# Attention with output projection, group norm and a masked 3x3 convolution: projection in three float16 products, statistics gathered over 60 units, mask tables built earlier

## What is computed

```python
x = x + L0(_gn(x), W_qkv, W_out, rel_height, rel_width)
x = x + L1(_gn(x), weight, bias)
```

## Time and profile before

| | us |
|---|---|
| median of 3 runs | 3703.85 |
| the profiled execution, its own time | 3702.19 |
| its span | 3700.4 |
| PE busy (share of the span) | 3491.4 (94%) |
| DVE busy | 3349.1 (91%) |
| ACT busy | 2966.0 (80%) |
| POOL busy | 2575.1 (70%) |

### The profile page before, as it was taken

How to read it: one execution, slowest core, us unless ns; L and a number is a source line. 1 busy time by engine, 2 the same in 40 slices (tenths; PEclk the granted TensorE clock), 3 DMA queues, 4 the chain that set the end, 5 groups by cost and what they waited for, 6 DMA issues and landing times. The chain is left out here.

```text
span 3700.4 us, 127356 instructions
## 1 busy us (share of the span) xinstructions
PE 3491.4 (94%) x51718; PEld 2480.6 (67%) x51718; DVE 3349.1 (91%) x5626; ACT 2966.0 (80%) x5320; POOL 2575.1 (70%) x3344
## 2 busy tenths in 40 slices
PE   0799999998999999999999999999589999999999
PEld 0587777777888888888888888888434444444444
DVE  9699999999999999999999999999789888888887
ACT  0788888887999999999999999998377777777774
POOL 1677777776777777777777777777366666666664
PEclk9999999999999999999999999999799999999999
DMA  8244544443333333333333333333244434344332
GB/s 374 79 132 133 159 134 154 148 139 105 103 103 97 94 98 103 103 97 91 101 103 103 95 91 103 103 100 83 69 160 162 154 146 154 147 154 154 154 154 83
DMA packets 492549, 464.06 MB, mean 125 GB/s; under 512 B 9664, under 2 KB 469312, under 8 KB 469440
## 3 DMA queue, kind: packets, MB, share of 16 engines
q1 hardware_dynamic: 491968, 455.92, 38.4%
HBM read 321.40 MB, written 134.48 MB: 123 GB/s over the span
## 5 line engine op out<-in xcount | busy, mean ns | idle before, releaser
L984 POOL TENSOR_TENSOR sb_tf<-sb_cf 128x1024 f32<-128x1024 f32 x256 | 609.4, 2382 | 392.2 <-DVE sb_tl L966 370.3
L450 PE MATMUL ps_t<-sb_ident,sb_d 128*108 128x128 f32 x4096 | 662.3, 284 | 6.2 <-ACT sb_pt L638 1.9
L600 DVE TENSOR_TENSOR sb_qb<-ps_q,sb_own_head 128x1024 f32<-128x1024 f32 x512 | 621.1, 1213 | 14.9 <-PE ps_q L432 14.9
L470 PEld LDWEIGHTS ps_s<-sb_kf,sb_qb 128*64 128x64 f32 x16384 | 519.1, 138 | 171.5 <-issue 162.9
L719 POOL TENSOR_TENSOR sb_erel<-sb_brel 128x288 f32<-128x288 f32 x512 | 351.5, 686 | 395.6 <-DVE sb_brel L547 394.7
L892 PE MATMUL ps_c<-sb_th,sb_wc_h 128*128 128x512 f16 x1536 | 584.3, 380 | 40.3 <-DVE sb_tl L966 40.2
L470 PE MATMUL ps_s<-sb_kf,sb_qb 128*64 128x54 f32 x16384 | 585.6, 224 | 2.4 <-DVE sb_scores L580 2.4
L892 PE MATMUL ps_c<-sb_th,sb_wc_l 128*128 128x512 f16 x1536 | 583.3, 380 | 0.0
L892 PE MATMUL ps_c<-sb_tl,sb_wc_h 128*128 128x512 f16 x1536 | 583.2, 380 | 0.0
L749 POOL TENSOR_TENSOR sb_zl<-sb_zf,sb_zh 128x396 f16<-128x396 f32 x512 | 481.1, 940 | 83.1 <-ACT sb_zh L702 83.1
L735 POOL TENSOR_TENSOR sb_prod<-sb_rel,sb_shift 128x192 f32<-128x192 f32 x1024 | 502.1, 511 | 0.0
(11 more groups left out here) (117 smaller groups left out, 8228.0 us busy)
## 6 DMA issues: line engine op xcount, KB each, us to landing
sb_xb<-rows SPq DMA_DIRECT2D x128, 780.0 KB, 6.5
sb_xc<-x SPq DMA_DIRECT2D x64, 1280.0 KB, 5.4
sb_x<-rows SPq DMA_DIRECT2D x128, 512.0 KB, 4.1
x<-sb_x SPq DMA_DIRECT2D x128, 512.0 KB, 3.3
out<-sb_oc SPq DMA_DIRECT2D x64, 1024.0 KB, 3.9
sb_abuf<-rows SPq DMA_DIRECT2D x16, 2048.0 KB, 11.7
sb_st<-rows SPq DMA_DIRECT2D x32, 1024.0 KB, 9.3
sb_raw<-wconv SPq DMA_DIRECT2D x1, 576.0 KB, 3.7
```

The costliest lines, as they stand in the source:

```text
L450: last = pe.transpose(ps_t[0:KV, wj * 128:(wj + 1) * 128], d[:, at:at + KV], ident[:])
L470: last = pe.matmul(s_at, qb[:, qc:qc + QB], kf[:, kc:kc + KR], start=True, stop=True)
L600: dve.tensor_tensor(view(qb, 0, 128, vh * QBW + p * NW * QB, [[QB, NW], [QN, HEADS], [1, QN]]), view(ps_q, 0, 128, 0, [[QN, NW], [0, HEADS ...
L984: pool.tensor_tensor(tf[:, k * TF:(k + 1) * TF], view(cf, 0, 128, c0 + ra * W, [[2 * W, PAIRROWS], [1, W]]), view(cf, 0, 128, c0 + rb * W, ...
```

## The change

The output projection: `wo` and `of` become float16 high and low halves. ACT's copy writes the high half `oh`; DVE makes the low half `ol` from `ps_o` and `oh`, in the body of each group right after `x1`, for group n-5; PE makes three products in place of one, and its `ps_o` of the next group waits for `ol` where it waited for `of`.

The statistics of batch 1: a load is now 4 rows (512 KB). Units 0 to 3 take two of them each, units 4 to 59 one each. SP issues it at the end of its body, behind the load of L413, and DVE takes its two pieces at the end of g = 3 of the same unit. The moments of batch 1 follow in unit 60.

The mask: the moments of L0's output for batch 0 are made in unit 70, and its tables in unit 71. Those for batch 1 are made at the start of the convolution's own block, beside its first loads. The zero rows are stored in unit 4. The two blocks between the stages are gone.

```diff
-        wo = sb("wo", C, F32)
+        wo_h, wo_l = sb("wo_h", C, F16), sb("wo_l", C, F16)
...
-        def moments_tables(dve, link, batches, sqrt_done):
+        def moments_tables(dve, link, batches, sqrt_done, edges=True):
...
+            if not edges:
+                return
...
+        def tile_extremes(dve, link, b):
+
+            hs, n = STRIPS // B, TR // B
+            for t, dst, op in ((tmax, ext[0], ALU.max), (tmin, ext[1], ALU.min)):
+                for h in range(2):
+                    link(dve.tensor_reduce(view(dst, 0, 128, b * n * TC + 4 * h, [[TC, n], [1, 4]]),
+                                           view(t, 0, 128, b * n * 8 * SPT + 4 * h, [[8 * SPT, n], [1, 4], [8, SPT]]),
+                                           AX.X, op))
+                part = tiles_of(dst, b)
+                link(dve.tensor_scalar(part, part, mean_t[:, b * hs:b * hs + 1],
+                                       rstd_t[:, STRIPS + b * hs:STRIPS + b * hs + 1], ALU.subtract, ALU.mult))
+
+            link(dve.scalar_tensor_tensor(tiles_of(ext[0], b), tiles_of(ext[1], b), -1.0, tiles_of(ext[0], b),
+                                          ALU.mult, ALU.max))
+
+        def row_tables(dve, link, b, all_channels):
+
+            hs, n, S8 = STRIPS // B, TR // B, CSTRIPS * TC
+            lo, hi = b * S8 // B, (b + 1) * S8 // B
+            rstd = rstd_t[:, STRIPS + b * hs:STRIPS + b * hs + 1]
+            dve.wait_ge(all_channels, 1)
+            link(dve.tensor_scalar(tiles_of(tabs, b), tiles_of(tabs, b), THRESHOLD, rstd, ALU.is_gt, ALU.mult))
+            for q in range(SPT):
+                dve.tensor_copy(view(ctab, 0, 128, S8 + lo + q * TC, [[SPT * TC, n], [1, TC]]),
+                                view(tabs, 0, 128, b * n * TC, [[TC, n], [1, TC]]))
+            dve.memset(ctab[:, lo:lo + TC], 0.0)
+            dve.memset(ctab[:, 2 * S8 + hi - TC:2 * S8 + hi], 0.0)
+            link(dve.tensor_scalar(nmean[:, b:b + 1], mean_t[:, b * hs:b * hs + 1], -1.0, None, ALU.mult))
+            dve.tensor_copy(ctab[:, lo + TC:hi], ctab[:, S8 + lo:S8 + hi - TC])
+            link(dve.tensor_copy(ctab[:, 2 * S8 + lo:2 * S8 + hi - TC], ctab[:, S8 + lo + TC:S8 + hi]))
+            link(dve.tensor_scalar(view(dtab, 0, 128, lo, [[S8, 3], [1, hi - lo]]),
+                                   view(ctab, 0, 128, lo, [[S8, 3], [1, hi - lo]]), nmean[:, b:b + 1], None, ALU.mult))
...
-                    dve.tensor_copy(wo[:], rawn[:, SPANS[1][0]:SPANS[1][1]])
+                    dve.tensor_copy(wo_h[:], rawn[:, SPANS[1][0]:SPANS[1][1]]).then_inc(w_qh, 1)
+                    dve.wait_ge(w_qh, 1)
+                    dve.tensor_tensor(wo_l[:], rawn[:, SPANS[1][0]:SPANS[1][1]], wo_h[:], ALU.subtract)
...
-                    dve.wait_ge(w_qh, 1)
+                    dve.wait_ge(w_qh, 2)
...
-            STW = WS * W
-            st = sb("st", 2 * STW, F32, pb)
...
+            st = sb("st", 2 * (WS // 2) * W, F32, pb)
...
-            of = sb("of", 2 * 1024, F32, pb)
+            oh, ol = sb("oh", 2 * 1024, F16, pb), sb("ol", 2 * 1024, F16, pb)
...
-            FIRST, LOOP = 6, 4
-            STRIPS_1 = STRIPS // B
-            EARLY = STRIPS_1 // LOOP
-            GN = FIRST + LOOP * EARLY
...
+            HALF = WS // 2 * W
+            HALVES = H * W // HALF
+            DOUBLE = 4
+
+            def gathered(u):
+
+                if 0 <= u < DOUBLE:
+                    return (2 * u, 2 * u + 1)
+                return (u + DOUBLE,) if DOUBLE <= u < HALVES - DOUBLE else ()
+
+            MOMENTS = {HALVES - DOUBLE: 1, UNITS // B + 6: 0}
+            MASK = UNITS // B + 7
             GROUP_STEPS = 2 + 5
...
-                    body(u, u // 2, u % 4, some,
-                         (u - FIRST, (u - FIRST) // 2) if FIRST <= u < GN else None, u == GN)
+                    body(u, u // 2, u % 4, some)
...
-                    if stat is not None:
-
-                        row = settled(sp, (stat[0] + STRIPS_1) * WS + PAD)
-                        sp.wait_ge(sem["st_used"], (stat[0] + 1) * PAR)
-                        sp.dma_start(st[:, h * STW:(h + 1) * STW],
-                                     x_in[:, bass.ds(row, WS), :].rearrange("p a b -> p (a b)")
-                                     ).then_inc(st_loaded[h], 16)
...
+                    for k in gathered(u):
+
+                        row = H + k * (WS // 2) + PAD
+                        if k >= 2:
+                            sp.wait_ge(sem["st_used"], 2 * (k - 1))
+                        sp.dma_start(st[:, k % 2 * HALF:(k % 2 + 1) * HALF],
+                                     x_in[:, row:row + WS // 2, :].rearrange("p a b -> p (a b)")
+                                     ).then_inc(st_loaded[k % 2], 16)
+                    if u == DOUBLE:
+
+                        sp.wait_ge(sem["zeroed"], 1)
+                        for row in (0, ROWS + 1):
+                            sp.dma_start(x1_dram[:, row:row + 1, :].rearrange("p a b -> p (a b)"), zrow[:]
+                                         ).then_inc(sem["edges"], 16)
                 units(sp, body)
                 sp.wait_ge(sem["x1_stored"], UNITS * 16)
+                sp.wait_ge(sem["edges"], 32)
...
-                    if moments_due:
-                        pe.wait_ge(sem["gn_agg_done"], 1)
-                        pe.matmul(ps_q[:, 0:2], gsum[:], aggr[:, 2:4], start=True, stop=True
-                                  ).then_inc(sem["gn_sum_done"], 1)
-                        pe.wait_ge(sem["gn_step_done"], GROUP_STEPS)
+                    if due is not None:
+                        pe.wait_ge(gn_sem[due]["agg_done"], 1)
+                        pe.matmul(ps_q[:, 0:2], gsum[:], aggr[:, 2 * due:2 * due + 2], start=True, stop=True
+                                  ).then_inc(gn_sem[due]["sum_done"], 1)
+                        pe.wait_ge(gn_sem[due]["step_done"], GROUP_STEPS)
...
-                            need(pe, sem["of_done"], m)
+                            need(pe, sem["ol_done"], m)
...
                             if g == 0:
-                                pe.wait_ge(sem["of_done"], (u - 1) * GROUPS)
+                                pe.wait_ge(sem["ol_done"], (u - 1) * GROUPS)
                             need(pe, sem["x1_done"], n - 2 * GROUPS)
                             ob = slot % 2
-                            pe.matmul(ps_y[:, 0:QP], wo[:], of[:, ob * 1024 + g * QP:ob * 1024 + (g + 1) * QP],
-                                      start=True, stop=True).then_inc(sem["y_mm"], 1)
+                            for c, (o, w) in enumerate(((oh, wo_h), (oh, wo_l), (ol, wo_h))):
+                                last = pe.matmul(ps_y[:, 0:QP], w[:], o[:, ob * 1024 + g * QP:ob * 1024 + (g + 1) * QP],
+                                                 start=(c == 0), stop=(c == 2))
+                            last.then_inc(sem["y_mm"], 1)
...
-                def stat_pieces(stat, h, first, count):
-
-                    if first == 0:
-                        dve.wait_ge(st_loaded[h], stat[1] * 16 + 16)
-                    for c in range(first, first + count):
-                        dve.bn_stats(stats[:, bass.ds(stat[0] * (PAR * 6) + (UNITS * 6 + c * 6), 6)],
-                                     st[:, h * STW + c * 512:h * STW + (c + 1) * 512]
-                                     ).then_inc(sem["st_used"], 1)
...
+                link = [linker(dve, gn_sem[b]["step_done"]) for b in range(B)]
...
-                        if moments_due and g == 1:
-                            moments_group(dve, link, (1,), ps_q, sem["gn_sum_done"])
+                        if u in MOMENTS and g == 1:
+                            b = MOMENTS[u]
+                            moments_group(dve, link[b], (b,), ps_q, gn_sem[b]["sum_done"])
+                        if on(n - 5, GT):
+
+                            v, vslot, vg = (u - 1, slot - 1, g - 1) if g else (u - 2, slot - 2, GROUPS - 1)
+                            dims = [[QP, PAR], [1, GW * QN]]
+                            dve.wait_ge(sem["oh_done"], n - 4)
+                            need(dve, sem["y_mm"], (v - 1) * PAR)
+                            dve.tensor_tensor(view(ol, 0, 128, (vslot % 2) * 1024 + vg * GW * QN, dims),
+                                              view(ps_o, 0, 128, 0, [[GW * QN, PAR], [1, GW * QN]]),
+                                              view(oh, 0, 128, (vslot % 2) * 1024 + vg * GW * QN, dims), ALU.subtract
+                                              ).then_inc(sem["ol_done"], 1)
...
-                        if stat is not None:
-                            if g != 1:
-                                stat_pieces(stat, h, (0, 4, 1, 2)[g], (1, 0, 1, 2)[g])
-                        if moments_due and g == 0:
-                            moments_sums(dve, link, (1,), sem["gn_agg_done"])
-                        if moments_due and g == 2:
-                            moments_tables(dve, link, (1,), sem["gn_sqrt_done"])
```

(65 more changed lines are left out.)

94 lines of the change are left out of this document (26 added, 68 removed).

## The result

The changed kernel takes 3809.68 us (median of 4 runs, 3807.32 to 3810.1) against 3703.78: ratio 1.0284, 95% interval 1.0267 to 1.0302. It is slower by 106 us. The forecast said 3742, range 3706 to 3792: the sign is right, the size is missed by 68 us and the range too.

What follows compares the result with a forecast made beforehand. TensorE bounds attention, DVE its statistics stretch; after the change DVE bounds all attention. Terms + 3, + 32, + 45, - 34, + 20, - 28.5, + 0.4 make + 38 on 3702.2: 3740, as median 3742 us, range 3706 to 3792.

Steps and rivals of the forecast that it cites:

- T + 5.2: Units 4 to 59: gathered load lands 5.2 us (at most 6.0) after T, the tile minimum's end; DVE waits 1.4 us.
- T + 3.9: Units 4 to 59: the 512 KB load queued ahead of the gathered one lands 3.9 us after the tile minimum's end.
- The estimate of 3.2 us: Gathered load, units 4 to 59: 2.0 us plus bytes at 436 GB/s, 3.2 us from issue, so DVE would not wait.
- Rival 2, the clock: TensorE's clock falls in each gathering unit, PE then needing 21.9 us against DVE's 21.35: + 31, 3773 us; chance 0.07.
- The reduction, 2.60 until its result is used: Mask tables in unit 71: POOL's reduction delays the relative part some 1.5 us, within 7.4 us for the block.
- E + 14.5: After attention: POOL's first row combination starts 14.5 us after E, the last tile minimum's end, instead of 43.0; 28.5 us gained.
- PE's unit goes to 18.5: Attention: three float16 projection products save PE 0.8 us a unit, from 19.30 to 18.5 us (at most 18.85).
- DVE becomes the bound everywhere in attention: With low halves DVE needs 18.76 us a unit, more than PE's 18.5, and 19.96 in units 4 to 59.
- the first one: Units 4 to 59: the gathered load lands in time, 80 us of waits go, 3662 us; chance 0.14.
- The third: Units from 60 on: engines don't even out between groups, a unit takes 19.55 us, + 50, 3792 us; chance 0.09.
- The fourth: Projection: three float16 products cost PE as much as the float32 one, 19.3 us from unit 60, 3776 us; chance 0.04.
- three limits that the prediction set for being wrong: Wait for sb_st under 0.75 us, clock in units 4 to 59 below 0.95, or period from unit 60 19.3 or more.

Runs made afterwards that it cites:

- e4: The changed kernel, with SP waiting until the gathered load has landed before it issues the next load of xb: 3795.99 us, ratio 1.0245.
- e3: The changed kernel with only the projection undone (one float32 product, float32 copy, no low half on DVE): 3771.05 us, ratio 1.018.
- e1: The changed kernel with SP issuing the gathered load right behind the load of xb, at the start of its body: 3684.99 us, ratio 0.9947.
- e2: The changed kernel with POOL's two late partition_all_reduce replaced by a tensor_tensor add of the same columns: 3792.15 us, ratio 1.0232.

## Why the prediction was wrong

In units 4 to 59 the mechanism was right: the order of the queues, the place of the wait and its releaser, and with them the low half (0.34) and DVE's unit with a gathered pair (19.94, forecast 19.96). The waiting there was put too low, and further terms were mis-sized; what bounds the units from 60 on was wrong (point 4).

1. **"It lands at T + 5.2 ... so DVE waits 1.4 us a unit."** Measured 1.93, and 0.53 x 56 = 30 us. The step that failed first is the landing of the load ahead, T + 3.9: I took the median of 20 transfers, where the mean of 52 between 240 and 1280 us of before is 4.14 and single ones reach 5.65. DVE has no reserve, so it pays each transfer's own delay and the mean counts, tail included. In the kernel after the mean is 4.18, which explains about 0.3 of the 0.5. The rest is the load's own part, 1.51 us between the two landings where I had taken 1.3. The load of xb behind has 0.18 in these two together (e4). The estimate of 3.2 us that the prediction took from the Trainium skill, "DMA: Bandwidth & Descriptors", section "Anatomy of one DMA — SWDGE (gpsimd) path", belongs to transfers issued by GpSimd, and these are issued by SP; by the 4.14 us for 512 KB it would have been too low for the load ahead as well. The upper end of my own range for the wait, 2.0, was near; the whole range missed because the other terms below went the same way with it.

2. **Rival 2, the clock.** It was kept apart from the forecast as all or nothing. It came in part: in 23 of 55 units the clock fell to 1.2 GHz, mostly for 3.4 us, and PE's spare time took most of it. Those units are 0.36 us longer besides their wait, 8 us in all, instead of 31; that the lower clock is what lengthens them is argued, since no run holds it alone. Between 240 and 1280 us of e3, with PE idle for 6% instead of 10%, it fell once; in e1, with 3%, never. The Trainium skill, "TensorE: Matmul & The Clock Gate", section "HAM oscillation — how this bites in real kernels", describes a clock that falls in every tile of such a loop. The direction agrees; that it falls in every unit, the trace does not bear out.

3. **"The reduction, 2.60 until its result is used, holds POOL ... for some 1.5", and "POOL's reduction 2.6, E + 14.5, and only then POOL's first row combination."** The 2.60 is what DVE waited for the result; what POOL itself loses ahead of and behind a reduction stood in no row that I had shown. It is 7.4 us at unit 71 and 6.5 at the end (e2): 5.9 over the forecast at the first place, nearly all of the excess in moments and mask, and most of the 7.3 at the end. The row was there. Timeline of POOL in the kernel before, stage A:

```profile
9.59 0.39 POOL L295 PARTITION_ALL_REDUCE sb_amax_all<-sb_amax  x1 [9.16 <-DVE sb_amax L255]
9.86 1.93 POOL L296 MEMSET sb_d<- 128x2112 f32 x1
13.85 0.50 POOL L301 COPY sb_gw<-sb_rawn 128x384 f32<-128x384 f32 x1 [2.06 <-DVE sb_rawn L271]
...
25.36 0.98 POOL L303 TENSOR_TENSOR sb_gw<-sb_rawn 128x384 f32<-128x384 f32 x1 [10.56 <-issue]
```

The first `tensor_tensor` behind that reduction waits 10.56 us for nothing shown, while a memset runs at once and the copies as soon as DVE has their data. Behind the late reduction of before POOL stood idle for 21.94 us anyway, waiting for ACT; that can hide the same. A step moved from an idle engine to a busy one has to be costed by what its engine does before and after it.

4. **"I take 0.11: 0.33 a group, a gain of 0.20 a group", "PE's unit goes to 18.5", and from it "DVE becomes the bound everywhere in attention".** The three products cost 0.42, not 0.33: the third takes 0.20 until the float32 product behind it starts, and the row of before for that step, `ps_v` to `ps_o`, is not in its working. PE gains 0.42 us a unit, half of the 0.8, and its unit is 18.89. DVE needs less than that, so from unit 60 TensorE bounds with no idle time to speak of, as before the change. That 18.89 lies so near to the forecast's 18.8 is luck: the two engines are nearly level. Units 60 to 126 took 18.89 on average, and 19.27 before, where I wrote 18.8 and 19.3: 9 us.

5. **Small ones.** Units 0 to 3 lost 8.1 instead of 3: I counted unit 3's double load alone, but all four gather two. Waits for the load have 2.2 us of it, in unit 3; e1, without them, has 77.7 us there. The base of units 4 to 59 was 5 us too high.

Together 30 + 8 + 5 for units 4 to 59, 6, 7, 9 and 5 - 1 at the start: 69 us, the distance from 38 to 107.

Of the rivals, the first one (the load is there in time) describes what e1 does, not this kernel. The third did not happen. The fourth, no gain for PE from the float16 products, came halfway: 0.42 us a unit of the forecast's 0.8. None of the three limits that the prediction set for being wrong was reached: the wait is over 0.75, the clock is 0.97, the period from unit 60 is 18.89. So they could not have shown this miss.
